# Decoder of two blocks on one core: shifts of the self attentions by blocks of eight heads, and a new table of turns

## Chip, cores, metric

One core of a Trainium2 chip runs the whole program in one launch; the other cores are idle. The metric is the time of one execution in microseconds, median of 3 runs.

## What is computed

Six layers with residuals over `x` of 4 batches, 256 tokens, 128 channels, each behind a layer norm:

```python
x = x + _L0_attn_ref(_layernorm(x), ...)            # 16 heads of 8, learned relative bias added after softmax
x = x + _L0_xattn_ref(_layernorm(x), ctx, ctx, ...) # 16 heads of 64, causal and padding masks
x = x + _L0_ffn_ref(_layernorm(x), ...)             # quantized linear, depthwise convolution, silu, quantized linear
x = x + _L1_attn_ref(_layernorm(x), ...)            # 16 heads of 4, causal, alibi
x = x + _L1_xattn_ref(_layernorm(x), ctx, ctx, ...) # attention between the 16 heads of each token
x = x + _L1_ffn_ref(_layernorm(x), ...)             # 8 experts, top 2, and a shared one
```

A self attention, of which the change speaks, is per batch and head

```python
attn = softmax(einsum('bhqd,bhkd->bhqk', q, k) * scale, axis=-1)
out = einsum('bhqk,bhkd->bhqd', attn + rel_bias, v)   # first block; the second has mask and alibi inside the softmax
```

## The kernel before

**Two lanes.** Lane A computes batches 0 and 1, lane B batches 2 and 3 (`NB` = 2 batches, `TT` = 4 tiles of 128 tokens each). Each lane has a region of SBUF, four PSUM banks (`bank[0]` to `bank[3]`, printed as A_banks and B_banks) and runs the stages l0a, l0x, ffn, l1a, l1x, moe one after the other. Weights and their quantization are a third program, W (`B_wq`), late loads a fourth, L.

**What sets the order.** Every stage gives one generator per engine; each `yield` ends a piece. `merged` (in `decoder`) joins the generators of an engine into its one queue by the string in `TURNS`: "A4 W1 A7" takes four pieces of lane A, one of the weights, seven of lane A. The numbers behind `yield` are not read by it (only `interleaved`, inside a stage, sorts by them). Engines wait for one another by semaphores, and nothing overtakes in a queue.

**Self attention, l0a and l1a** (class `Attention`, L176 to L358; the stages `rel_attention` and `alibi_attention`).

1. Normalization: VectorE takes statistics, GpSimd the power (`rstd`, L159), VectorE applies it (L164). TensorE transposes the tokens (L172), and at the very start of l0a also the context (L633), which a DMA brings (L464).
2. Projection per token tile (L647). Queries and keys are split into three bf16 parts each by VectorE (L566, L569) and GpSimd (L487, L490), then stacked in the rows of `stack`, queries by GpSimd (L496), keys by ScalarE (L531). TensorE transposes the stacks (L662, 16 steps `n` of four), and they are copied to `qkT` by VectorE (L459) or, every fourth, by ScalarE (L511). GpSimd clears the stack's space and `vals` beforehand (L477 to L482). In l1a the stacks are transposed at L1585 and copied at L1491 and L1495.
3. Maxima: TensorE computes scores with queries in rows (`tensor_S_pair` L296 for the first 16 heads of l0a, two heads at a time in both halves of the array; `tensor_S`, L226, for the others; L231 and L234 in l1a), VectorE takes minus the maximum of each row (L324). `JOBS` is 16 in l0a and 12 in l1a per batch.
4. Shift: when all 16 heads of a batch have their maximum, VectorE splits it into three bf16 parts (`vector_parts`, L339 to L348), TensorE transposes them (L242), VectorE copies (`vector_shiftT`, L352), and SP sends them by DMA into three rows of the queries (`sync_shift`, L252), so that the next scores come out with the maximum subtracted.
5. Loop over `U` = 32 heads: scores with keys in rows (L310; L262 to L266 in l1a), exponential on ScalarE (L358), products with the values per four heads (L286), output transposed and normalized.

```python
self.s_mx = st.sem("max_done", NB * self.JOBS)
if h == 0:
    pe.wait_ge(*self.s_q(16 * self.G * (b + 1)))
done, now = (min(jobs, k * jobs // (H - EARLY)) for k in (h, h + 1))
```

The first batch's maxima all stand before the loop; those of the second batch are spread over the first twelve heads of the loop (`ahead`, L361, with `EARLY` = 4), and its shift follows at head 12.

## Time and profile before

| | us |
|---|---|
| runs | 624.28, 620.47, 622.31 |
| median | 622.31 |
| the profiled execution's own time | 619.47 |
| its span | 617.5 |
| TensorE busy | 529.0 |
| VectorE busy | 424.6 |
| ScalarE busy | 323.5 |
| GpSimd busy | 192.1 |
| mean granted TensorE clock | 0.954 |

The span is from the first to the last instruction of the profiled execution; its own time is 2 us more. Busy times are of instructions that work; waits for semaphores and issuing of DMAs are not in them. The idle time of an engine is the span less its busy time.

### The profile page before, as it was taken

The page shows a single profiled execution, that of the slowest core. Times are in us where ns is not written, and L with a number is a line of the kernel's source. Part 1 is how long each engine was busy: PE and PEld are TensorE (multiplying, and loading weights), DVE is VectorE, ACT ScalarE, POOL GpSimd, SP SyncE. Part 2 cuts the span into 40 slices and gives each one's busy share as a digit, 9 for nine tenths or more (in the row PEclk, how much of TensorE's full clock was granted, in tenths as well). Part 3 has the DMA queues.
Part 4 walks back from the last instruction along what each step waited for, and adds up shares of the span by engine and source line. Part 5 has one row for each costly group of instructions (what it writes and reads, how often), then busy time and mean ns, then how long its engine had stood idle before and what let it go on. Part 6 is the DMA issues. An engine that isn't in the chain of part 4 may idle for free. (4 is left out here: it accounts for less than half of the span.)

```text
span 617.5 us, 12861 instructions
## 1 busy us (share of the span) xinstructions
PE 529.0 (86%) x4880; PEld 327.9 (53%) x4890; DVE 424.6 (69%) x1037; ACT 323.5 (52%) x807; POOL 192.1 (31%) x288
## 2 busy tenths in 40 slices
PE   2668787999999999778986489978988999999894
PEld 1433343344555656446554355766666867655453
DVE  6885764654463654798779876847557577889994
ACT  1423445567576674695733536554666555362440
POOL 3743200043245443432620031001113122435653
PEclk9965999999999999989997889999999999999998
DMA  8700000000030000000256005300000000303001
GB/s 299 267 1 2 2 2 3 1 3 2 1 136 3 1 1 1 2 2 1 80 143 243 3 17 156 97 11 3 4 2 2 3 3 1 138 2 137 2 1 34
DMA packets 25815, 27.92 MB, mean 45 GB/s; under 512 B 18177, under 2 KB 22794, under 8 KB 24858
## 3 DMA queue, kind: packets, MB, share of 16 engines
q1 hardware_dynamic: 25754, 27.10, 13.1%
q8 instruction: 39, 0.64, 0.4%
q14 instruction: 22, 0.18, 0.1%
HBM read 22.14 MB, written 4.75 MB: 44 GB/s over the span
## 5 line engine op out<-in xcount | busy, mean ns | idle before, releaser
L811 POOL TENSOR_TENSOR A_l0x_prob<-A_l0x_prob,A_l0x_inverted_sums 128x256 f32<-128x256 f32 (+1 forms) x32 | 25.9, 829 | 56.6 <-DVE A_l0x_inverted_sums L922 56.6
L811 POOL TENSOR_TENSOR B_l0x_prob<-B_l0x_prob,B_l0x_inverted_sums 128x256 f32<-128x256 f32 (+1 forms) x32 | 26.5, 848 | 45.1 <-DVE B_l0x_inverted_sums L922 45.1
L2080 PE MATMUL B_banks<-B_moe_xT,w_moe_rows 128*128 128x512 f32 x72 | 33.8, 596 | 1.7 <-DVE B_moe_h L2047 1.7
L2080 PE MATMUL A_banks<-A_moe_xT,w_moe_rows 128*128 128x512 f32 x72 | 34.3, 597 | 0.0
L324 DVE TENSOR_REDUCE B_l0a_nmax<-B_banks 128x2 f32<-128x512 f32 x32 | 21.4, 688 | 15.2 <-PE B_banks L226 11.9
L905 DVE TENSOR_REDUCE A_l0x_nmax<-A_banks 128x2 f32<-128x256 f32 (+1 forms) x32 | 16.3, 552 | 22.6 <-PE A_banks L980 22.5
L358 ACT ACTIVATE A_l0a_expT<-A_banks 128x512 f32<-128x512 f32 x32 | 18.3, 599 | 22.0 <-PE A_banks L310 22.0
L829 ACT ACTIVATE B_l0x_prob<-B_banks,B_l0x_nmax 128x128 f32<-128x128 f32 x64 | 26.0, 420 | 5.9 <-DVE B_l0x_nmax L905 5.7
L324 DVE TENSOR_REDUCE A_l0a_nmax<-A_banks 128x2 f32<-128x512 f32 x32 | 21.3, 688 | 9.8 <-PE A_banks L226 8.0
L829 ACT ACTIVATE A_l0x_prob<-A_banks,A_l0x_nmax 128x128 f32<-128x128 f32 x64 | 26.1, 425 | 1.7 <-DVE A_l0x_nmax L905 1.7
L846 ACT ACTIVATE A_l0x_probT<-A_banks 128x384 f32<-128x384 f32 x32 | 15.8, 493 | 19.3 <-PE A_banks L992 19.1
L846 ACT ACTIVATE B_l0x_probT<-B_banks 128x384 f32<-128x384 f32 x32 | 15.7, 490 | 15.9 <-PE B_banks L992 15.8
L324 DVE TENSOR_REDUCE B_l1a_nmax<-B_banks 128x2 f32<-128x512 f32 (+1 forms) x24 | 16.2, 689 | 9.9 <-PE B_banks L234 9.7
L358 ACT ACTIVATE B_l0a_expT<-B_banks 128x512 f32<-128x512 f32 x32 | 18.6, 601 | 8.2 <-PE B_banks L310 8.1
L358 ACT ACTIVATE A_l1a_expT<-A_banks 128x384 f32<-128x384 f32 x32 | 15.3, 494 | 14.5 <-PE A_banks L266 14.5
L358 ACT ACTIVATE B_l1a_expT<-B_banks 128x384 f32<-128x384 f32 x32 | 15.5, 491 | 14.0 <-PE B_banks L266 13.9
L1976 ACT ACTIVATE B_moe_h<-B_banks,w_moe_rest_rows 128x512 f32<-128x512 f32 x18 | 12.3, 686 | 19.7 <-PE B_banks L2080 19.6
L2080 PEld LDWEIGHTS B_banks<-B_moe_xT,w_moe_rows 128*128 128x128 f32 x72 | 12.8, 190 | 14.7 <-issue 12.0
L905 DVE TENSOR_REDUCE B_l0x_nmax<-B_banks 128x2 f32<-128x256 f32 (+1 forms) x32 | 16.2, 548 | 5.9 <-PE B_banks L980 5.9
L1709 POOL TENSOR_TENSOR A_l1x_prob<-A_l1x_prob,A_l1x_rz 128x512 f32<-128x512 f32 x8 | 8.3, 1042 | 38.2 <-DVE A_l1x_rz L1790 38.2
L1976 ACT ACTIVATE A_moe_h<-A_banks,w_moe_rest_rows 128x512 f32<-128x512 f32 x18 | 12.1, 680 | 13.8 <-PE A_banks L2080 13.7
L992 PE MATMUL B_banks<-w_const_rows,B_l0x_prob 128*128 128x128 f32 x96 | 16.6, 283 | 3.0 <-POOL B_l0x_prob L811 1.4
(609 smaller groups left out, 1570.7 us busy)
## 6 DMA issues: line engine op xcount, KB each, us to landing
w_toeplitz_rows<-in_toeplitz_rows SPq DMA_DIRECT2D x1, 3072.0 KB, 15.3
w_moe_rows<-in_moe_rows SPq DMA_DIRECT2D x1, 2304.0 KB, 9.6
w_l1x_rows<-in_l1x_rows SPq DMA_DIRECT2D x1, 2048.0 KB, 7.8
A_l1x_values<-A_l1a_v_tokens SPq DMA_DIRECT2D x4, 512.0 KB, 3.5
A_l1x_v_groups<-A_l1x_values SPq DMA_DIRECT2D x16, 128.0 KB, 3.1
B_l1x_values<-B_l1a_v_tokens SPq DMA_DIRECT2D x4, 512.0 KB, 3.5
B_l1x_v_groups<-B_l1x_values SPq DMA_DIRECT2D x16, 128.0 KB, 3.1
w_l0x_vo_rows<-in_l0x_vo_rows SPq DMA_DIRECT2D x1, 1024.0 KB, 9.0
```

Of the source, the lines that this page charges most:

```text
L324: dve.tensor_reduce(out, scores, AX, ALU.max, negate=True).then_inc(self.s_mx.sem, 1)
L358: act.activation(self.expT[:, u % self.ring, :], self.exp_bank(u)[:, 0:self.W], ACT.Exp, scale=self.scale).then_inc(self.s_p.sem, 1)
L811: ins = pool.tensor_tensor(pair, pair, bcast(rz[:, g % 2, i, :], 2, n), ALU.mult)
L829: ins = act.activation(prob[:, u % RING, at:at + n], bank[u % 2][:, at:at + n], ACT.Exp, bias=nmax[:, b, i, h:h + 1], accum_out=zsum[:, g ...
L846: act.activation(probT[:, u % 4, :], bank[2][:, 0:W], ACT.Copy).then_inc(s_pt.sem, 1)
L905: ins = dve.tensor_reduce(nmax[:, b, i, 2 * c:2 * c + 2], lane.banks[:, 0:2, at:at + n], AX, ALU.max, negate=True)
L992: ins = pe.transpose(bank[2][:, c * P:(c + 1) * P], prob[:, u % RING, c * P:(c + 1) * P], w["ident"][:])
L1709: pool.tensor_tensor(pr, pr, bcast(rz[:, n % 2, :], BL, 64), ALU.mult).then_inc(s_pn.sem, 1)
L1976: act.activation(h1[:, n % 2, :], hidden_bank(2 * n)[:, :], ACT.Identity, bias=w["moe_b1"][:, e, part:part + 1]).then_inc(s_h1.sem, 1)
L2080: pe.matmul(hidden_bank(k)[:, :], w["moe_w3" if which else "moe_w1"][:, ORDER[i], part, :], xT[:], start=True, stop=True).then_inc(s_h.sem, 1)
```

## The change

- **Blocks of eight heads** (`HB` = 8) take the place of batches in the shift: maxima, parts, transpose, copy and DMA are done for each of 4 blocks per lane and stage (`JOBS` is 8 in l0a, 6 in l1a, per block). `parts` and `shiftT` are double buffers over the blocks, with waits for their reuse.
- **How far ahead**: `due(n)` says how many score sets are issued by step `n` of the loop, `AHEAD` = 12 heads ahead. Before the loop stand `first` = 12 sets in l0a and 9 in l1a, of which the last 4 (3) come behind the first block's shift. A later block's shift is sent four steps before its first exponential.
- `tensor_S_pair` is gone; all heads' maxima scores come from `tensor_S`.
- **Stack copies** of the steps from `n` = 8 on are all ScalarE's (10 of 16 instead of 4); each is issued behind one set of scores.
- **Start of l0a**: TensorE transposes the tokens ahead of the context, ScalarE copies them in that order, and the context goes through `bank[3]`; the wait for it moves to the second stack transpose. GpSimd clears `vals` and the stack first and then computes `rstd`.
- **New turns** for all engines. Operations outside the two self attentions are the same; ScalarE's queue gets 10 table loads where it had 8.

```diff
-EARLY = 4
+HB = 8
+AHEAD = 12
...
-        self.jobs = [job for h in range(0, H, 4) for job in ((1, h, 2), (1, h + 2, 2), (0, h, 4))] if causal else [(None, h, 1) for h in range(H)]
+        self.jobs = [job for h in range(0, HB, 4) for job in ((1, h, 2), (1, h + 2, 2), (0, h, 4))] if causal else [(None, h, 1) for h in range(HB)]
+        self.BLOCKS = U // HB
+        self.first = self.due(-1)
...
+    def due(self, n):
+
+        return min(self.BLOCKS * self.JOBS, -(-(n + 1 + AHEAD) * self.JOBS // HB))
...
+    def completed(self, n):
+
+        k = self.due(n) // self.JOBS
+        return k - 1 if n >= 0 and k * self.JOBS > self.due(n - 1) else None
...
+        rows, n = P // self.G, HB // self.G
+        b, first = k * HB // H, k * HB % H // self.G
         for j in range(self.G):
-            dst = self.queries(b)[rows * j + self.row:rows * j + self.row + 3]
-            src = self.shiftT[32 * j:32 * j + 3 * self.columns, b, :]
+            dst = self.queries(b)[rows * j + self.row:rows * j + self.row + 3, first:first + n, :]
+            src = self.shiftT[32 * j:32 * j + 3 * n, k % 2, :]
             sp.dma_start(dst, src).then_inc(self.s_q.sem, 16)
...
-        if h == 0:
-            pe.wait_ge(*self.s_q(16 * self.G * (b + 1)))
+        if u % HB == 0:
+            pe.wait_ge(*self.s_q(16 * self.G * (u // HB + 1)))
+        if u == 0:
+            pe.wait_ge(*self.s_mx(self.first))
...
-    by_scalar = [n % 4 == 3 for n in range(STEPS)]
+    by_scalar = [n % 4 == 3 or n >= 4 * SB for n in range(STEPS)]
...
     def gpsimd(pool):
-        yield 2.0
-        w.loaded(pool, "const")
+        yield 0.0
         w.ready(pool, lane, "arena")
-        norm.gpsimd_rstd(pool)
-        yield 1.6
-        w.ready(pool, lane, "x")
-        yield 2.1
+        pool.memset(vals[:], 0.0).then_inc(s_init.sem, 1)
         pool.memset(stack[:, :, 0, :, 6 * HD:SW], 0.0)
...
+        yield 2.0
+        w.loaded(pool, "const")
+        norm.gpsimd_rstd(pool)
...
     def tensor(pe):
-        yield 0.0
+        yield 4.5
         w.loaded(pe, "const")
         w.ready(pe, lane, "arena")
+        tensor_transpose_tiles(pe, w, bank[0], xn, s_xn, s_xTp)
+        yield 5.5
         pe.wait_ge(*s_ctx(16))
...
-            if u % 2 == 0:
-                a.tensor_S_pair(pe, u)
-            else:
+            if u == a.JOBS:
+                a.tensor_shift(pe, 0)
+                yield SCORES + 1.2 * u + 0.8
+            a.tensor_S(pe, u)
+            if 4 * SB + u < STEPS:
                 yield
-                transpose_stack(4 * SB + u // 2)
+                transpose_stack(4 * SB + u)
...
-        "A4 W1 A7 W1 A20 B1 A4 B1 A1 B1 A3 B1 A3 B1 A3 B1 A1 B1 A1 B1 A3 B1 A2 B2 A3 B1 A2 B2 A5 B2 A2 B1 A3 B1 A2 B2 A5 B3 A2 B3 A3 B1 A3 B1 A1 B4 A4 B1 A2 B2 "
+        "A4 W1 A5 W1 A20 B1 A1 B1 A2 B1 A2 B1 A6 B2 A3 B1 A1 B2 A4 B1 A4 B1 A1 B1 A1 B1 A3 B1 A5 B2 A3 B3 A1 B1 A2 B1 A1 B1 A1 B2 A3 B3 A2 B1 A4 B1 A1 B1 A6 B1 "
...
```

The table of turns moves most instructions. Three places, each of before and of the change, rows as they stand in the queue of the engine (names of the program's tiles; `x4` is four in a row):

GpSimd's queue from lane A's third token tile on, before (`split` the parts of queries and keys, `expT` the space in which the stacks are built, `vals` the values, `rstd` the norm's factor):

```order
L487 CAST A_l0a_split<-A_l0a_rest_qk 128x256
L490 TENSOR_TENSOR A_l0a_split<-A_l0a_rest_qk,A_l0a_split 128x256
L496 COPY A_l0a_expT<-A_l0a_split 128x16x16 x2
L496 COPY A_l0a_expT<-A_l0a_split 128x16x8 x2
L159 TENSOR_TENSOR B_l0a_rstd<-B_l0a_ve,w_const_rows 128x4
L487 CAST A_l0a_split<-A_l0a_rest_qk 128x256
L490 TENSOR_TENSOR A_l0a_split<-A_l0a_rest_qk,A_l0a_split 128x256
L496 COPY A_l0a_expT<-A_l0a_split 128x16x16 x2
L496 COPY A_l0a_expT<-A_l0a_split 128x16x8 x2
L477 MEMSET B_l0a_expT 128x4x16x16
L478 MEMSET B_l0a_expT 128x4x16x13
```

and with the change:

```order
L499 CAST A_l0a_split<-A_l0a_rest_qk 128x256
L502 TENSOR_TENSOR A_l0a_split<-A_l0a_rest_qk,A_l0a_split 128x256
L484 MEMSET B_l0a_vals 128x3072
L485 MEMSET B_l0a_expT 128x4x16x16
L486 MEMSET B_l0a_expT 128x4x16x13
L487 MEMSET B_l0a_expT 128x4x16x3
L489 MEMSET B_l0a_vals 128x64
L508 COPY A_l0a_expT<-A_l0a_split 128x16x16 x2
L508 COPY A_l0a_expT<-A_l0a_split 128x16x8 x2
L499 CAST A_l0a_split<-A_l0a_rest_qk 128x256
L502 TENSOR_TENSOR A_l0a_split<-A_l0a_rest_qk,A_l0a_split 128x256
```

Lane B's five clears now stand between the split of lane A's third tile and its stack, and lane B's `rstd` behind the split of the fourth.

TensorE's queue around the first shift of lane A, before (`parts` the shift's parts, L242 its transpose, L310 the exponentials' scores, L226 and L296 the maxima's, L662 stack transposes, L647 the projection):

```order
L296 MATMUL A_banks<-A_l0a_qkT 128x256 x4
L647 MATMUL B_banks<-w_l0a_rows,B_l0a_xT 128x384
L662 MATMUL A_banks<-w_ident_bf,A_l0a_expT 128x128 x4
L242 MATMUL A_banks<-w_ident_bf,A_l0a_parts 128x128 x2
L647 MATMUL B_banks<-w_l0a_rows,B_l0a_xT 128x384
L310 MATMUL A_banks<-A_l0a_qkT 128x256 x4
L226 MATMUL A_banks<-A_l0a_qkT 128x256 x2
L662 MATMUL B_banks<-w_ident_bf,B_l0a_expT 128x128 x4
```

and with the change (L264 the shift's transpose, L327 the exponentials' scores, L248 the maxima's, L677 stack transposes, L660 the projection):

```order
L677 MATMUL A_banks<-w_ident_bf,A_l0a_expT 128x128 x4
L248 MATMUL A_banks<-A_l0a_qkT 128x256 x2
L173 MATMUL B_banks<-w_const_rows,B_l0a_xn 128x128 x4
L677 MATMUL A_banks<-w_ident_bf,A_l0a_expT 128x128 x4
L649 MATMUL B_banks<-w_const_rows,B_l0a_rest_qk 128x128 x4
L264 MATMUL A_banks<-w_ident_bf,A_l0a_parts 128x128 x2
L248 MATMUL A_banks<-A_l0a_qkT 128x256 x2
L660 MATMUL B_banks<-w_l0a_rows,B_l0a_xT 128x384
L248 MATMUL A_banks<-A_l0a_qkT 128x256 x4
L660 MATMUL B_banks<-w_l0a_rows,B_l0a_xT 128x384
L248 MATMUL A_banks<-A_l0a_qkT 128x256 x2
L327 MATMUL A_banks<-A_l0a_qkT 128x256 x4
```

The shift is transposed behind eight sets of scores, and four more sets, one head each, stand between it and the first exponentials.

ScalarE's queue where lane A's experts begin beside lane B's second cross attention (`moe_sigmoid` needs another table of functions than `l1x_prob`), before:

```order
L1740 ACTIVATE B_l1x_probT<-B_banks 128x512
L1744 ACTIVATE B_l1x_prob<-B_l1x_prob 128x512
L1982 ACT_TABLE_LOAD
L1982 ACTIVATE A_moe_sigmoid<-A_moe_gate 128x512
L1976 ACTIVATE A_moe_h_165<-A_banks,w_moe_rest_rows 128x512 x2
L1733 ACTIVATE B_l1x_keysT<-B_banks 128x4x128
```

and with the change:

```order
L1763 ACTIVATE B_l1x_prob<-B_l1x_prob 128x512
L2001 ACT_TABLE_LOAD
L2001 ACTIVATE A_moe_sigmoid<-A_moe_gate 128x512
L1995 ACTIVATE A_moe_h_165<-A_banks,w_moe_rest_rows 128x512
L1752 ACTIVATE B_l1x_keysT<-B_banks 128x4x128
L1759 ACTIVATE B_l1x_probT<-B_banks 128x512
L1763 ACT_TABLE_LOAD
L1763 ACTIVATE B_l1x_prob<-B_l1x_prob 128x512
```

An exponential of lane B (L1763) now stands behind lane A's first sigmoid, with a table load before it, and the next sigmoid takes another.

## Rows read from the trace of the kernel before

**Rows 1.** Part 1 of the page: engine busy us (share of the span) xinstructions.
```profile
PE 529.0 (86%) x4880; PEld 327.9 (53%) x4890; DVE 424.6 (69%) x1037; ACT 323.5 (52%) x807; POOL 192.1 (31%) x288
```

**Rows 2.** Windows: stretch, length, busy us (xinstructions) by engine, PEclk, DMA share, GB/s.
```profile
0.00:50.00 50.00, 26.71 (x169) 15.97 (x170) 36.01 (x87) 15.55 (x42) 27.92 (x54) 0.85 0.49 175
50.00:100.00 50.00, 41.69 (x429) 20.31 (x429) 30.91 (x75) 23.27 (x56) 6.25 (x14) 0.84 0.01 2
300.00:350.00 50.00, 36.34 (x266) 23.72 (x265) 40.29 (x103) 21.91 (x58) 11.52 (x38) 0.92 0.46 144
```

**Rows 3.** Timeline of TensorE, 0 to 50 us: start us, us, what [idle before].
```profile
9.71 1.09 PE L633 MATMUL A_banks<-w_const_rows,A_l0a_rest_qk 128*128 128x128 f32 x4 [9.71 <-DMA A_l0a_rest_qk<-in_ctx]
...
13.01 2.90 PE L647 MATMUL A_banks<-w_l0a_rows,A_l0a_xT 128*128 128x384 f32 x4 [0.78 <-ACT A_l0a_xT L518]
...
43.43 0.27 PE L242 MATMUL A_banks<-w_ident_bf,A_l0a_parts 128*128 128x128 bf16 x2 [0.73 <-ACT A_l0a_qkT L511]
...
47.24 0.39 PE L310 MATMUL A_banks<-A_l0a_qkT 64*128 64x256 bf16 x4 [2.83 <-DMA A_l0a_qkT<-A_l0a_shiftT]
```

**Rows 4.** Timeline of VectorE, 0 to 50 us.
```profile
6.79 4.77 DVE L164 TENSOR_SCALAR A_l0a_xn<-A_x,A_l0a_mv,A_l0a_rstd 128x128 f32<-128x128 f32 x4
...
26.32 1.29 DVE L324 TENSOR_REDUCE A_l0a_nmax<-A_banks 128x2 f32<-128x512 f32 x2
...
27.52 0.41 DVE L459 COPY A_l0a_qkT<-A_banks 128x512 bf16<-128x512 bf16 x1
...
41.07 1.29 DVE L324 TENSOR_REDUCE A_l0a_nmax<-A_banks 128x2 f32<-128x512 f32 x2 [0.37 <-PE A_banks L296]
...
43.74 0.29 DVE L352 COPY A_l0a_shiftT<-A_banks 128x256 bf16<-128x256 bf16 x1 [0.16 <-PE A_banks L242]
```

**Rows 5.** Timeline of GpSimd, 0 to 30 us.
```profile
5.70 1.05 POOL L159 TENSOR_TENSOR A_l0a_rstd<-A_l0a_ve,w_const_rows 128x4 f32<-128x4 f32 x1 [5.26 <-DVE A_l0a_ve L155]
...
6.71 0.94 POOL L477 MEMSET A_l0a_expT<- 128x1024 bf16 x1
...
11.46 0.23 POOL L482 MEMSET A_l0a_vals<- 128x64 f32 x1
...
23.87 1.21 POOL L496 COPY A_l0a_expT<-A_l0a_split 128x256 bf16<-128x256 bf16 x4
...
28.59 1.21 POOL L496 COPY A_l0a_expT<-A_l0a_split 128x256 bf16<-128x256 bf16 x4
```

**Rows 6.** Timeline of VectorE, 110 to 115 us.
```profile
112.76 1.11 DVE L164 TENSOR_SCALAR A_l0a_xn<-A_l0a_xn,A_l0a_mv,A_l0a_rstd 128x128 f32<-128x128 f32 x4
```

**Rows 7.** Timeline of VectorE, 325 to 350 us.
```profile
328.99 1.71 DVE L1495 COPY A_l1a_kT<-A_banks 32x512 bf16<-32x512 bf16 x4
...
348.41 0.29 DVE L352 COPY A_l1a_shiftT<-A_banks 128x256 bf16<-128x256 bf16 x1
```

**Rows 8.** Timeline of TensorE, 350 to 355 us.
```profile
352.91 0.40 PE L262 MATMUL A_banks<-A_l1a_qT,A_l1a_kT 128*128 128x256 bf16 x1 [1.01 <-DMA A_l1a_qT<-A_l1a_shiftT]
```

**Rows 9.** Timeline of TensorE, two places in lane A's first loop.
```profile
64.14 0.39 PE L226 MATMUL A_banks<-A_l0a_qkT 64*128 64x256 bf16 x2
64.46 0.44 PE L706 MATMUL A_banks<-w_const_rows,A_l0a_xT 128*128 128x128 f32 x2
...
88.88 0.39 PE L296 MATMUL B_banks<-B_l0a_qkT 64*128 64x256 bf16 x4
89.11 0.38 PE L310 MATMUL A_banks<-A_l0a_qkT 64*128 64x256 bf16 x4
```

**Rows 10.** Timeline of ScalarE, 340 to 342 us.
```profile
340.00 1.28 ACT L1114 ACT_TABLE_LOAD   x1
341.30 1.72 ACT L1114 ACTIVATE B_ffn_conv<-B_ffn_conv 128x512 f32<-128x512 f32 x3
```

**Rows 11.** Tiles A_l0a_qkT and A_l0a_shiftT: durations ns min/median/max, first and last start us.
```profile
L310 PE MATMUL A_banks<-A_l0a_qkT x64: 266/279/417, 47.2 to 98.3; 64*128 64x256 bf16 x64
...
L252 SPq DMA_DIRECT2D A_l0a_qkT<-A_l0a_shiftT x4: 698/710/887, 44.1 to 76.3; - x4
```

More of the change, by code:

```diff
@@ L216, in tensor_S @@
     def tensor_S(self, pe, m):
-        b, at = divmod(m, self.JOBS)
-        c, h, n = self.jobs[at]
+        b, c, h, n = self.job(m)
         bank = self.score_bank(m)
-        if b:
+        if m == self.JOBS or m >= self.first:
             pe.wait_ge(*self.s_mx(m))
@@ L223, in tensor_S @@
             pe.wait_ge(*self.s_mx(m - 1))
+        if self.shifted is not None and bank is self.bank[0]:
+            pe.wait_ge(*self.s_shT(self.shifted + 1))
+            self.shifted = None
         if c is None:
@@ L288, in tensor_PV @@
         ins.then_inc(self.s_pv.sem, 1)
-    def tensor_S_pair(self, pe, m):
-        if m:
-            pe.wait_ge(*self.s_mx(m))
-        for c in range(SB):
-            for h in (m, m + 1):
-                ins = pe.matmul(self.score_bank(h)[:, c * S:(c + 1) * S], self.q(0, h, c * P, P), self.k(0, h, 0, S),
-                                start=(c == 0), stop=True, skip_group_check=True)
-                if c == SB - 1:
-                    ins.then_inc(self.s_s.sem, 1)
     def tensor_E_pair(self, pe, u):
         b, h = divmod(u, H)
-        if h == 0:
-            pe.wait_ge(*self.s_q(16 * self.G * (b + 1)))
+        if u % HB == 0:
+            pe.wait_ge(*self.s_q(16 * self.G * (u // HB + 1)))
+        if u == 0:
+            pe.wait_ge(*self.s_mx(self.first))
         if u:
@@ L315, in vector_max @@
     def vector_max(self, dve, m):
[L316 to L317 removed]
+        b, c, h, n = self.job(m)
         bank = self.score_bank(m)
@@ L358, in scalar_exp @@
         act.activation(self.expT[:, u % self.ring, :], self.exp_bank(u)[:, 0:self.W], ACT.Exp, scale=self.scale).then_inc(self.s_p.sem, 1)
-def ahead(n, jobs):
-    b, h = divmod(n, H)
-    if b + 1 >= NB:
-        return range(0)
-    done, now = (min(jobs, k * jobs // (H - EARLY)) for k in (h, h + 1))
-    return range(jobs * (b + 1) + done, jobs * (b + 1) + now)
 def split_columns(part_of):
@@ L535, in scalar @@
                 copy_stack(act, scalar_copy, 4 * t - 1)
-        for n in (STEPS - 5, STEPS - 1):
-            yield SCORES + 1.2 * (2 * n - 4 * TT + 1) + 0.2
+        for n in range(4 * SB, STEPS):
+            yield SCORES + 1.2 * (n - 4 * SB) + 0.8
             copy_stack(act, scalar_copy, n)
@@ L671, in tensor @@
                     transpose_stack(n)
-        for u in range(a.JOBS):
+        for u in range(a.first):
             yield SCORES + 1.2 * u - 0.4
@@ L694, in tensor @@
                 a.tensor_E_pair(pe, n)
-            for i, u in enumerate(ahead(n, a.JOBS)):
+            for i, u in enumerate(range(a.due(n - 1), a.due(n))):
                 yield LOOP + STEP * (n + 0.5 * i) - 0.5
@@ L1348, in sync @@
                     sp.dma_start(vg[64 * half:64 * (half + 1), to:to + P // 16, :], src[half, j]).then_inc(s_vg, 16)
-        for b in range(NB):
-            yield SCORES + 3.0 + 0.75 * a.JOBS + 2.0 if b == 0 else LOOP + STEP * (b * H - EARLY + 1)
-            a.sync_shift(sp, b)
+        for k in range(a.BLOCKS):
+            yield SCORES + 3.0 + 0.75 * a.JOBS + 2.0 if k == 0 else LOOP + STEP * (k * HB - 3)
+            a.sync_shift(sp, k)
     def gpsimd(pool):
@@ L1587, in tensor @@
             ins.then_inc(s_stT.sem, 1)
-        for u in range(a.JOBS):
+        for u in range(a.first):
             yield SCORES + 3.0 + 0.75 * u - 0.4
@@ L1604, in tensor @@
                 a.tensor_E(pe, n)
-            for i, u in enumerate(ahead(n, a.JOBS)):
+            for i, u in enumerate(range(a.due(n - 1), a.due(n))):
                 yield LOOP + STEP * (n + 0.5 * i) - 0.5
```

166 lines of the change are left out of this document (89 added, 77 removed), and 42 rows, old and new, of the table TURNS.

## Prediction

> **What bounds the kernel now.** I read the engine shares first: TensorE is busy for 86% of the span [rows 1], so beside it everything else is mostly cover, and the other 88.5 us (617.5 - 529.0) are all that a better order can win back. Then the stretches [rows 2] say where they lie: TensorE does 26.7 us of work in the first 50 us and 41.7 in the next 50, at a mean granted clock of 0.85 and 0.84; from 300 to 350, where both lanes stand around the second self attention, only 36.3. So 31.6 us of the idle time lie before 100 us and 13.7 in 300 to 350, over half of it in a quarter of the span. The chain of waits that ends the program is of no use here: it reaches back only over the last 14 us. What decides are the starts of the two self attentions, in which one lane has little to do and the other has not caught up.
>
> Lane A's start is a serial story [rows 3]. TensorE first waits 9.71 us for the context tokens, projects from 13.01, and after the last of 16 score sets transposes the shift at 43.43; the first matmul of the loop of exponentials comes at 47.24, after 2.83 us of waiting for the shift's DMA. In between VectorE sets the pace [rows 4]: 8 pairs of maxima from 26.32 to 42.36, 2.0 us a pair, 1.29 of it the two maxima and 0.41 the stack copy that stands in the same queue. GpSimd [rows 5] clears lane A's buffers after the first rstd (6.71 to 11.69), and while it does so VectorE's four normalizations take 4.77 us [rows 4]; the same four take 1.11 us later [rows 6].
>
> **The change part by part**, as lane A meets it.
>
> 1. *Buffers cleared ahead, tokens ahead of the context.* The five clears (4.98 us, [rows 5]) move in front of rstd. GpSimd has nothing before 5.70, so they end about when x's variance is there, and rstd keeps its time. The normalizations no longer run beside them: 6.79 + 1.11 = 7.9 instead of 11.56. But the context is still transposed before the first projection on TensorE's queue and still lands at 9.71; its four transposes take 1.09 [rows 3], so the projection starts near 10.8 instead of 13.01: **-2.2 us** on this chain. Token transposes and xT (ScalarE) are done by then.
>
> 2. *GpSimd's new turn for lane B's clears.* Before, lane B's clears follow all four q stacks of lane A, the last of which ends at 29.80 [rows 5]. Now they stand between the split and the stack of lane A's third token tile. That stack would end 2.2 us earlier than 25.08, at 22.9; the clears are the same five as lane A's, 4.98, so it ends near 27.9, the fourth (4.72 us behind it before, 29.80 - 25.08, of which some waiting for its split falls away, while lane B's rstd, 1.05 like lane A's, is put in between) near 31. Every score set but the first is queued on TensorE behind a stack transpose of these tiles, so the scores cannot run ahead of them.
>
> 3. *Eight maxima instead of sixteen before the shift, and ScalarE copies the stacks.* Eight maxima at 0.65 (1.29/2) are 5.2 us, with no copy between. Sets 4 to 7 follow the fourth stack at 31: the last maximum ends near 34.5 where it ended at 42.36. Parts, transpose and shift copy then take what they took (42.39 to 44.03), the DMA its 3.2 us (47.24 - 44.03), although it carries half the bytes; I take no gain from these. **The loop starts near 39.5 instead of 47.24: -7.7 us.** Four sets and their maxima (0.3 us of TensorE each) move from before it into the loop or under the DMA: +0.7, leaving **-7.0**. Bounds: -4 if lane B's clears wait for the quantized weights and push the stacks on, -10 if the stacks don't hold the scores.
>
> 4. *Lane B's start.* It has the same 4 sets fewer, but lane A's loop fills TensorE beside it (41.7 of 50). I count **-1** (0 to -4).
>
> 5. *Second self attention.* From the end of the key copies (330.7) to the shift copy (348.41) VectorE is full: 12 maxima, lane B's FFN and the parts [rows 7], while TensorE waits; its loop opens at 352.91 [rows 8]. Six maxima (6 x 0.65 = 3.9) leave this stretch for the loop, where VectorE should have idle time as in the first one (30.9 of 50 us busy beside lane A's first loop, [rows 2]). Lane B's convolution steps move ahead of the stack copies, which changes their place, not the sum. **-4** for lane A, **-1** for lane B, whose stretch has less idle time. Bounds for both: 0 and -7.
>
> 6. *What it adds.* Each stage and lane has two shifts more. TensorE: 16 transposes, two of them in 0.27 us [rows 3], **+2**. VectorE: two more blocks of four or five small operations and a copy, about 1.2 us a block if a small one takes 0.2 and the copy 0.29 [rows 4]; the first self attention gives 6 stack copies of 0.41 back per lane, so it adds nothing there, and 2.4 per lane in the second, under TensorE. 24 more DMAs on SP, 0.7 us each to issue [rows 11], on a queue that is nearly empty; none of them stands behind one that lands late except in the second self attention, where lane A's last two blocks queue behind lane B's value transfers.
>
> 7. *Unpaired scores.* The score sets of the first 16 heads came in pairs, four matmuls whose halves of the array overlap; now each head comes alone. In the loop of before two single matmuls hold TensorE for 0.32 us (64.14 to 64.46), four paired ones for 0.23 (88.88 to 89.11) [rows 9]. A pair of heads so costs 0.64 instead of 0.23 to 0.33. 16 pairs in both lanes: 16 x 0.35 = 5.6, of which lane A's half falls into idle time; **+2.5**.
>
> 8. *Two more table loads on ScalarE*, where lane A's experts start inside lane B's cross attention. A load takes 1.28 us, and the activation behind it starts 0.02 us later [rows 10]: 2.6 us on an engine that is busy half the time; I count 0 (bounds 0 and +2.6). The Trainium skill, "ScalarE: Activation LUTs", section "What ACT_TABLE_LOAD costs", counts a drain of some 1.38 us on top, 2.66 us a switch; the sum's upper bound by it would be +5.3, but the row shows no drain.
>
> Sum: -7.0 - 1 - 4 - 1 + 2 + 2.5 = **-8.5 us**. Against the profiled execution (span 617.5, its own time 619.47) that is 611.0; the median of the three runs is 622.31, 2.8 above it, so the same sum gives 613.8 for the median; between the two, and nearer the second, since it is medians that are compared, I say **613**. About 0.5% (3 us) is what a measurement of this kernel can tell from no change.
>
> **Rivals.**
> *R1, only the first start counts* (0.17). If the second attention's stretch stays bound by VectorE's same sum of work (B's FFN chain ends no earlier, and its extra 5 us of small operations land there), item 5 falls out: -8.5 + 5 = -3.5, 618.8 for the median. For it: VectorE is busy 9 of 10 there; against it: the six maxima really leave.
>
> *R2, the idle time is only moved and TensorE pays* (0.12). TensorE gets 2 + 5.6 us more work. If the lanes wait as long as before, because each block's shift is one more round trip (maximum, parts, transpose, copy, 3.2 us DMA) in front of TensorE's queue, four instead of two per lane and stage, the time is 619.5 + 7.6 = 627 for the profiled execution, 630 for the median, and 626 if half of the extra work is hidden. It decides if TensorE's idle time before 100 us stays over 29 us. Against it: in the loop a block's exponentials come four heads after its maxima, 6.4 us at 1.6 us a head (32 heads from 47.2 to 98.3, [rows 11]), and the round trip takes about 5.
>
> *R3, the whole order gets tighter* (0.15). The new turns are laid for all stages; if the lanes' better alignment also takes 5 to 8 us of the idle time in 250 to 450 us and at the end, 601 to 607. For it: idle time there is larger than what I use; against it: nothing in the operations of these stages changes.
>
> *R4, the change is not what it says*: the order of instructions shows eight-head blocks in both lanes and stages, so nothing is left for it.
>
> **Numbers.** My forecast has 0.56: its own range is 608 to 618. R3 takes the low end to 603, R1 with the small ends of items 3 and 5 (3.7 and 5 us less gained, so none is left) the high end to 623; R2 and the bottom of R3 are left out: 603 to 623. Faster by over 0.5% (below 619.2): 0.56, all of R3 and a third of R1, 0.76. Within 0.5% : 0.13. Slower (over 625.4): 0.11.
>
> **What would show it.** TensorE's first exponential matmul of lane A near 39.5 us, not 47.2; the first four normalizations 1.1 us in sum; TensorE's idle time before 100 us near 24 us; lane A's second loop some 12 us earlier than 352.9; TensorE's busy time up by 3 to 7 us. I am wrong if the stacks hold the scores past 37 us, or if the gain of the start is gone by 150 us because lane B arrives no earlier.

## The result, and the profile after

| | before | with the change |
|---|---|---|
| median of 4 runs, us | 622.24 | 614.23 |
| lowest to highest | 620.47 to 624.28 | 612.85 to 615.70 |
| ratio, 95% interval | | 0.987, 0.9832 to 0.9909 |
| the profiled execution's own time | 619.47 | 615.70 |
| its span | 617.5 | 613.9 |
| mean granted TensorE clock in it | 0.954 | 0.956 |

The spans of the two profiled executions are only 3.6 us apart, the medians 8.0: the profiled execution of before is faster than all runs of its column, the one after is the slowest of its own. That is itself a part of the result (the clock, below).

The first lines of the profile after: engine busy us, share of the span, xinstructions.

```profile
PE 533.2 (87%) x4906; PEld 330.1 (54%) x4906; DVE 426.0 (69%) x1069; ACT 330.8 (54%) x821; POOL 195.2 (32%) x288
```

TensorE has 4.2 us more to do than in [rows 1] and is idle 80.7 us instead of 88.5. The windows before 100 us (columns as in [rows 2]):

```profile
0.00:50.00 50.00, 31.71 (x190) 17.80 (x190) 32.97 (x87) 21.67 (x55) 28.16 (x54) 0.85 0.48 175
50.00:100.00 50.00, 41.81 (x449) 20.81 (x451) 32.60 (x82) 26.24 (x59) 6.28 (x14) 0.84 0.01 3
```

Idle time before 100 us fell from 31.6 to 26.5 us (50 - 31.71 + 50 - 41.81). Further on, windows of fixed times cut the two programs at different work. So the next ones are cut at three places of the program: where lane A's first loop opens, where lane B issues the last scores of its first loop, and where lane A's second loop opens. Before:

```profile
0.00:47.24 47.24, 24.77 (x153) 14.98 (x154) 34.46 (x84) 13.73 (x37) 26.04 (x49) 0.86 0.51 186
47.24:158.04 110.80, 100.02 (x916) 46.82 (x918) 64.16 (x170) 60.73 (x149) 21.61 (x38) 0.92 0.01 2
158.04:352.91 194.87, 166.97 (x1214) 104.19 (x1212) 135.87 (x359) 119.55 (x375) 66.77 (x112) 0.96 0.15 49
352.91:617.47 264.56, 237.22 (x2602) 161.96 (x2610) 190.09 (x424) 129.52 (x247) 77.70 (x90) 0.98 0.11 36
```

and with the change:

```profile
0.00:42.20 42.20, 24.90 (x144) 14.54 (x145) 27.48 (x73) 16.59 (x42) 25.28 (x46) 0.88 0.57 207
42.20:160.94 118.74, 108.30 (x974) 52.63 (x974) 72.51 (x198) 69.24 (x176) 24.59 (x44) 0.91 0.01 2
160.94:346.82 185.88, 159.23 (x1155) 99.02 (x1151) 130.38 (x347) 113.53 (x355) 66.89 (x109) 0.98 0.16 51
346.82:613.92 267.10, 240.82 (x2638) 163.90 (x2638) 195.67 (x454) 131.45 (x249) 78.49 (x90) 0.97 0.11 35
```

TensorE is idle 22.5, 10.8, 27.9 and 27.3 us in the four stretches before, and 17.3, 10.4, 26.7 and 26.3 now. So 5.2 of the 7.8 us stand ahead of lane A's first loop, 0.3 in the next stretch, 1.2 ahead of the second loop and 1.1 behind. Work moves too: up to lane B's last scores TensorE is busy 8.4 us more than before, in the stretch behind 7.7 us less.

TensorE at lane A's start, in its order of time, answers to [rows 3]:

```profile
7.36 1.16 PE L173 MATMUL A_banks<-w_const_rows,A_l0a_xn 128*128 128x128 f32 x4 [7.36 <-DVE A_l0a_xn L165]
10.29 1.11 PE L649 MATMUL A_banks<-w_const_rows,A_l0a_rest_qk 128*128 128x128 f32 x4 [1.77 <-DMA A_l0a_rest_qk<-in_ctx]
11.19 2.77 PE L660 MATMUL A_banks<-w_l0a_rows,A_l0a_xT 128*128 128x384 f32 x4
...
27.29 0.40 PE L677 MATMUL A_banks<-w_ident_bf,A_l0a_expT 128*128 128x128 bf16 x4 [3.26 <-POOL A_l0a_expT L508]
...
33.32 0.61 PE L677 MATMUL A_banks<-w_ident_bf,A_l0a_expT 128*128 128x128 bf16 x4
33.87 0.61 PE L248 MATMUL A_banks<-A_l0a_qkT 64*128 64x256 bf16 x2
...
35.48 1.11 PE L173 MATMUL B_banks<-w_const_rows,B_l0a_xn 128*128 128x128 f32 x4
...
37.67 0.42 PE L264 MATMUL A_banks<-w_ident_bf,A_l0a_parts 128*128 128x128 bf16 x2
...
40.92 0.39 PE L248 MATMUL A_banks<-A_l0a_qkT 64*128 64x256 bf16 x2 [0.40 <-DVE A_l0a_nmax L340]
42.20 0.39 PE L327 MATMUL A_banks<-A_l0a_qkT 64*128 64x256 bf16 x4 [0.89 <-DVE A_l0a_nmax L340]
```

The projection starts at 11.19 (13.01 before), the shift's transpose at 37.67 (43.43), the loop at 42.20 (47.24). GpSimd and VectorE in the same stretch, against [rows 5] and [rows 4]:

```profile
21.27 2.66 POOL L484 MEMSET B_l0a_vals<- 128x3072 f32 x1
...
26.03 1.21 POOL L508 COPY A_l0a_expT<-A_l0a_split 128x256 bf16<-128x256 bf16 x4
...
29.25 1.22 POOL L508 COPY A_l0a_expT<-A_l0a_split 128x256 bf16<-128x256 bf16 x4
```

```profile
6.87 1.11 DVE L165 TENSOR_SCALAR A_l0a_xn<-A_x,A_l0a_mv,A_l0a_rstd 128x128 f32<-128x128 f32 x4
...
23.33 2.57 DVE L156 TENSOR_SCALAR B_l0a_ve<-B_l0a_mv 128x4 f32<-128x4 f32 x1
...
35.59 0.69 DVE L340 TENSOR_REDUCE A_l0a_nmax<-A_banks 128x2 f32<-128x512 f32 x1 [0.39 <-PE A_banks L248]
```

In the second self attention lane A's loop opens at 346.82 ([rows 8]: 352.91):

```profile
341.97 0.37 PE L264 MATMUL A_banks<-w_ident_bf,A_l1a_parts 128*128 128x128 bf16 x2 [2.84 <-DVE A_l1a_parts L367]
346.82 0.40 PE L288 MATMUL A_banks<-A_l1a_qT,A_l1a_kT 128*128 128x256 bf16 x1 [2.02 <-DMA A_l1a_qT<-A_l1a_shiftT]
```

### The profile page after: what moved, and what is told of

Read it like the earlier page. It is cut to its first block, busy times and chain, and to the rows that moved or that the text cites. A ratio compares the mean times of both kernels' runs of the same rounds, so it can differ in the third digit from the quotient of the medians.

```text
span 613.9 us, 13013 instructions
## 1 busy us (share of the span) xinstructions
PE 533.2 (87%) x4906; PEld 330.1 (54%) x4906; DVE 426.0 (69%) x1069; ACT 330.8 (54%) x821; POOL 195.2 (32%) x288
## 3 DMA queue, kind: packets, MB, share of 16 engines
q1 hardware_dynamic: 25826, 27.10, 13.4%
## 4 chain that ended last, share of the span: by engine, by line
PE 64%; DVE 19%; ACT 6%; issue 4%; POOL 2%; DMA 2%; SPq 1%; POOLq 0%; DVEq 0%; ACTq 0%
PE B_banks L2099 5%; PE A_banks L2099 4%; PE A_banks L312 4%; PE B_banks L312 3%; PE A_banks L1021 2%; PE A_banks L1008 2%; DVE A_l0a_nmax L340 2%; PE A_banks L248 2%; PE A_banks L2131 1%; PE B_banks L1562 1%; PE A_banks L1824 1%; PE A_banks L957 1%; PE A_banks L1029 1%; PE A_banks L959 1%; PE B_banks L957 1%
## 5 line engine op out<-in xcount | busy, mean ns | idle before, releaser
L340 DVE TENSOR_REDUCE B_l0a_nmax<-B_banks 128x2 f32<-128x512 f32 x32 | 21.8, 686 | 15.3 <-PE B_banks L248 15.1
L862 ACT ACTIVATE A_l0x_probT<-A_banks 128x384 f32<-128x384 f32 x32 | 15.7, 492 | 15.6 <-PE A_banks L1008 15.5
L340 DVE TENSOR_REDUCE A_l1a_nmax<-A_banks 128x2 f32<-128x512 f32 (+1 forms) x24 | 16.3, 687 | 8.2 <-PE A_banks L256 8.2
L1995 ACT ACTIVATE B_moe_h<-B_banks,w_moe_rest_rows 128x512 f32<-128x512 f32 x18 | 12.2, 685 | 17.3 <-PE B_banks L2099 17.2
```

The costliest lines, as they stand in the source:

```text
L340: dve.tensor_reduce(out, scores, AX, ALU.max, negate=True).then_inc(self.s_mx.sem, 1)
L862: act.activation(probT[:, u % 4, :], bank[2][:, 0:W], ACT.Copy).then_inc(s_pt.sem, 1)
L1995: act.activation(h1[:, n % 2, :], hidden_bank(2 * n)[:, :], ACT.Identity, bias=w["moe_b1"][:, e, part:part + 1]).then_inc(s_h1.sem, 1)
```

## Experiments

The variants were measured on three chips, each beside the kernel before, whose median is 622.5 to 622.6 on every one of them; "the changed kernel" below is its second measurement, made on one of the three. **The changed kernel again**, for comparison:

> The changed kernel unaltered, as the measure for the variants on the same chip: 614 us, 0.985 to 0.991 of the kernel before.

Measured 614.05 (613.15 to 616.50), ratio 0.9884 (0.9854 to 0.9914). Lane A's first loop opens at 42.99 in its profile and the second at 347.5. So a start time of two executions of one kernel differs by 0.8 us, and smaller differences are not read below. From the opening of the second loop to the end both profiles take 267.1 us (spans 613.9 and 614.6).

### The blocks: nothing behind the shift

```diff
+    if lane.name == "A":
+        a.shift_at = a.first        # twelve sets instead of eight
...
-            if u == a.JOBS:
+            if u == a.shift_at:
                 a.tensor_shift(pe, 0)
...
+        if a.shift_at == a.first:
+            a.tensor_shift(pe, 0)
```

(the same for the parts and the copy on VectorE)

> The changed kernel with lane A's first shift in the first self attention behind all twelve sets of scores that stand before the loop, not behind eight. Theory of the blocks: what the blocks of eight heads give is that the sets behind the shift cover its way (parts, transpose, copy, 3.2 us of DMA); now nothing covers it, lane A's first exponential scores come 3.5 to 4 us later (46), and the time is 2 to 4 us more. Rival, it is the new turns and stack copies that give the start, and the block's size little: first exponential scores within 1.5 us of 42.2 and the time within 1 us.

Measured 620.87 (617.91 to 624.31), 6.8 above the changed kernel, ratio 0.9977 (0.9957 to 0.9998) to the one before. Its timeline of TensorE:

```profile
44.04 0.28 PE L265 MATMUL A_banks<-w_ident_bf,A_l0a_parts 128*128 128x128 bf16 x2 [1.48 <-DVE A_l0a_parts L368]
47.81 0.61 PE L328 MATMUL A_banks<-A_l0a_qkT 64*128 64x256 bf16 x4 [3.48 <-DMA A_l0a_qkT<-A_l0a_shiftT]
```

The loop opens 4.8 us later and TensorE stands 3.48 us before it for the DMA, which no set of scores covers. With the new turns and the new stack copies in place, lane A's first shift alone, put behind four more sets, takes nearly the whole gain back. The theory of the blocks holds, and was priced too low (2 to 4). But not all of the 6.8 is the block's. Some 2 us are the clock (mean over the runs 0.952, 0.959 in those of the changed kernel, at the 3.0 us per 0.01 found below). The profiles say the same in another way. Against the repeated run lane B's last scores of the first loop come 4.2 us later (166.05, 161.90), and that is the delay of the start; lane A's second loop opens 7.9 us later (355.47, 347.53), which is also the difference of the spans (622.5, 614.6). The 3.8 us between the two were lost on the way: 189.4 us from the one place to the other, where the changed kernel takes 185.9 and 185.6. Two more variants below, whose first loops open no later than the repeated run's, lose as much there (189.6 and 189.8). All three have 6.8 us at half clock (granted clock 0.50) at about 300 us, here

```profile
299.70:306.50 6.80, 5.68 (x35) 4.07 (x34) 3.88 (x17) 2.31 (x4) 1.76 (x3) 0.50 0.00 0
```

where the repeated run of the changed kernel has none:

```profile
288.40:343.00 54.60, 41.81 (x308) 25.70 (x306) 47.61 (x133) 27.33 (x74) 15.74 (x41) 1.00 0.41 127
```

So the sets behind the first shift are worth 4 to 5 us, and the rest of the 6.8 goes with a lower clock, which a changed order can bring without a later start. Whether the half clock is all of those 3.8 us was not tried.

> The changed kernel with lane A's first shift in the second self attention behind all nine sets that stand before the loop, not behind six. In the changed kernel the last of six maxima ends at 339.8, the loop opens at 346.8. Theory: three maxima of 0.65 us and what stands between them on VectorE move ahead of the shift, the loop opens 2 to 4 us later, the time is 1 to 3 us more. Rival, VectorE's sum of work in this stretch bounds it, and the order within it does not matter: the loop opens within 1 us of 346.8, the same time.

The same edit in the second self attention (lane A, nine sets instead of six). Measured 618.78 (615.42 to 623.91), 4.7 above. TensorE there:

```profile
344.50 0.29 PE L265 MATMUL A_banks<-w_ident_bf,A_l1a_parts 128*128 128x128 bf16 x2 [3.79 <-DVE A_l1a_parts L368]
349.27 0.40 PE L289 MATMUL A_banks<-A_l1a_qT,A_l1a_kT 128*128 128x256 bf16 x1 [4.48 <-DMA A_l1a_qT<-A_l1a_shiftT]
```

and its window:

```profile
300.00:350.00 50.00, 34.66 (x245) 21.32 (x243) 41.56 (x108) 22.26 (x53) 12.07 (x37) 0.95 0.47 144
```

The loop opens at 349.3 instead of 346.8 to 347.5, and TensorE is idle 15.3 us in this window instead of 11.6. From there on the program takes 267.1 us, as the changed kernel. So the profiles give the block of the second self attention 1.8 to 2.5 us (span 616.4 against 614.6 and 613.9); of the 4.7 between the medians some 1 is the clock (0.955 against 0.959), and the rest isn't explained. The order within VectorE's work matters; the rival falls.

### Clears, and what stands behind a late instruction

Lane A's clears behind its rstd again:

```diff
-        pool.memset(vals[:], 0.0)...; norm.gpsimd_rstd(pool)
+        norm.gpsimd_rstd(pool); pool.memset(vals[:], 0.0)...      # lane A only
```

> The changed kernel with lane A's five clears behind its rstd again, as before the change (lane B's stay where the change has them). Start theory: rstd stays near 5.7, the clears run beside the four normalizations of lane A, which take 4.8 us instead of 1.1; the projection starts at 13.0 instead of 11.2 and the first exponential scores 1.8 us later, the time is 1 to 2 us more: 615.5 to 616. Rival, it is hidden by what follows (GpSimd's stacks, lane B's clears): first exponential scores within 0.5 us of 42.2, 614.

Measured 618.45 (616.55 to 621.73), 4.4 above the changed kernel. VectorE's row of the normalizations:

```profile
6.82 4.48 DVE L165 TENSOR_SCALAR A_l0a_xn<-A_x,A_l0a_mv,A_l0a_rstd 128x128 f32<-128x128 f32 x4
```

4.48 us instead of 1.11, the projection at 12.8, the loop at 43.8. The mechanism is as I had it. The median moved by more than the start did, of which some 1.3 us go by the clock (0.955 against 0.959); the span of the profile is 1.0 us longer (615.6, 614.6).

Lane B's clears and rstd behind lane A's stacks (two pieces of lane B moved in the table of GpSimd's turns):

```diff
     "gpsimd":
-        "A11 B1 A3 B1 A2 B14 ...
+        "A15 B2 A1 B14 ...
```

> The changed kernel with lane B's five clears and its rstd on GpSimd's queue behind the stack of lane A's fourth token tile. In the changed kernel the clears run from 21.27 to 26.03 and the stack behind them ends at 27.2, with TensorE waiting 3.26 us for it. Queue theory: the third stack now ends near 22.5, the fourth near 26.5, the first exponential scores of lane A come at 39 to 40 instead of 42.2, and the time is 1 to 3 us below the changed kernel (611 to 613). Rival, the lead is lost to lane B, whose clears and rstd now end 2 to 3 us later, so that its normalizations and its loop start later: same time as the changed kernel, 614. Rival, TensorE sets the pace anyway (a transposed stack and a set of scores every 1.08 us at half clock): lane A's first scores move by less than 1 us.

Measured 617.99 (614.11 to 620.26), 3.9 above, with the loop opening at 44.92: none of the three. The stacks were done early, and then this, on TensorE and on VectorE:

```profile
25.04 0.38 PE L677 MATMUL A_banks<-w_ident_bf,A_l0a_expT 128*128 128x128 bf16 x4 [0.92 <-ACT A_l0a_vals L537]
...
35.55 0.61 PE L248 MATMUL A_banks<-A_l0a_qkT 64*128 64x256 bf16 x2 [5.22 <-DVE A_l0a_nmax L340]
```

```profile
32.83 2.06 DVE L165 TENSOR_SCALAR B_l0a_xn<-B_x,B_l0a_mv,B_l0a_rstd 128x128 f32<-128x128 f32 x4 [5.71 <-POOL B_l0a_rstd L160]
```

Lane B's normalizations stand on VectorE's queue between lane A's third and fourth maximum. Their rstd was now late, and lane A's maxima, ready to run, waited 5.7 us behind them. So I moved those too, behind the parts of lane A's first shift on VectorE, and lane B's transposes behind that shift and the ninth set on TensorE, whose queue changes like this:

```diff
 L677 MATMUL A_banks<-w_ident_bf,A_l0a_expT 128x128 x4
+L264 MATMUL A_banks<-w_ident_bf,A_l0a_parts 128x128 x2
+L248 MATMUL A_banks<-A_l0a_qkT 128x256 x2
 L173 MATMUL B_banks<-w_const_rows,B_l0a_xn 128x128 x4
 L649 MATMUL B_banks<-w_const_rows,B_l0a_rest_qk 128x128 x4
-L264 MATMUL A_banks<-w_ident_bf,A_l0a_parts 128x128 x2
-L248 MATMUL A_banks<-A_l0a_qkT 128x256 x2
```

> As in the run with lane B's clears behind lane A's stacks, and besides lane B's normalizations on VectorE behind the parts of lane A's first shift, and lane B's token and context transposes on TensorE behind that shift and one set of scores. Head-of-line theory: the 5.7 us that lane A's maxima lost in that run came only from lane B's normalizations standing before them on VectorE's queue while their rstd was late. Now the eighth maximum ends near 33.3, the first exponential scores of lane A come at 39 to 40 (42.2 in the changed kernel), lane B's tokens are transposed at 35.5 as there, and the time is 1 to 3 us below the changed kernel. Rival, lane A's lead is worth nothing since lane B fills TensorE later: first exponential scores at 39 to 40, and the time of the changed kernel. Rival, stacks and clears were not what held lane A: first exponential scores at 42.

Measured 617.03 (612.66 to 617.36), ratio 0.9909 (0.9876 to 0.9941), which overlaps the changed kernel's. In its profile the shift is transposed at 34.18 (38.33 in the repeated run of the changed kernel), and lane B issues the last scores of its first loop at 158.9 (161.9), 3.0 us ahead. But lane A's second loop opens at 348.7 (347.5), and these are its windows, and then the repeated run's:

```profile
250.00:300.00 50.00, 37.61 (x281) 25.48 (x283) 39.46 (x101) 31.54 (x92) 17.06 (x24) 0.90 0.00 1
300.00:350.00 50.00, 36.62 (x253) 22.86 (x253) 41.46 (x108) 23.32 (x54) 11.68 (x37) 0.93 0.48 145
```

```profile
250.00:300.00 50.00, 36.78 (x298) 24.75 (x296) 40.80 (x104) 32.82 (x98) 16.48 (x23) 0.97 0.00 1
300.00:350.00 50.00, 38.35 (x264) 23.97 (x264) 43.39 (x117) 23.36 (x55) 12.52 (x37) 0.93 0.47 145
```

Up to 300 us the clock is lower (0.90, 0.97), up to 350 TensorE is idle 13.4 us instead of 11.6. The lead is gone before the second loop: this is the second of the variants with 6.8 us at half clock near 300 us (189.8 us from lane B's last scores to lane A's second loop, 185.6 in the repeated run). The head-of-line theory is right about the start (the eighth maximum ends at 32.72, and the transpose comes 4.1 us earlier), and the rival right about the time: a lead of 3 us at 160 us isn't carried to the end here. The loop itself opened at 41.45 only, not at 39 to 40, since the last of the twelve maxima now waits for sets that stand behind lane B's projections.

### The added work, the copies, the table loads

Every transpose of a shift three times:

```diff
-            ins = pe.transpose(view[...], self.parts[:, k % 2, c, :], ...)
+            for again in range(3):
+                ins = pe.transpose(view[...], self.parts[:, k % 2, c, :], ...)
```

> The changed kernel with every transpose of a shift issued three times, 64 more transposes on TensorE than the change has. At 0.13 us each (0.27 us for two) they are 8.6 us of TensorE. If TensorE bounds the program all through the loops: +7 to +9 us, 621 to 623, and the 16 transposes of the change cost 2 us as I summed them. If they fall into idle time of the starts or under waits for banks: +3 to +5, and they cost about 1.

Measured 616.64 (615.70 to 619.66), 2.6 above for 64 transposes, and less than either forecast; the interval of its ratio, 0.992 (0.9894 to 0.9946), overlaps the changed kernel's. But these transposes stand in groups that are there anyway. All shifts' transposes together are busy 4.93 us in the repeated run (32 of them) and 9.60 here (96): 0.07 us for one more in a group, not 0.13. The change adds groups: eight of two transposes, and TensorE's rows of them go from 2.24 to 5.07 us. So the run shows that a longer group is cheap, and not that the change's 16 transposes are.

Score pairs head by head, in the kernel before:

```diff
-        for c in range(SB):
-            for h in (m, m + 1):
+        for h in (m, m + 1):
+            for c in range(SB):
```

> The kernel before with the two heads of a score pair one after the other (the same matmuls, order head by head), which takes the overlap of the two halves of the array away and nothing else. My term: 16 pairs in both lanes at 0.35 us, lane A's half hidden, +2.5 us, 624.5 to 625; TensorE's busy time up by up to 5.6 us. Lower bound: the pairs wait for the maxima anyway, no difference (622). Upper bound: +5.6.

Measured 622.31 (619.69 to 624.43), ratio 1.0 (0.9981 to 1.002): the lower bound. TensorE is busy 529.8 us instead of 529.0, and the same row of its timeline, in this kernel and then in the one before:

```profile
26.16 0.40 PE L296 MATMUL A_banks<-A_l0a_qkT 64*128 64x256 bf16 x4 [0.97 <-ACT A_l0a_qkT L511]
```

```profile
25.91 0.39 PE L296 MATMUL A_banks<-A_l0a_qkT 64*128 64x256 bf16 x4 [0.97 <-ACT A_l0a_qkT L511]
```

Four matmuls take 0.40 us one head after the other and 0.39 paired. Two take 0.39 ([rows 9]): in so short a group the time is the same whatever the number. The Trainium skill ("TensorE: Matmul & The Clock Gate", section "Step-by-step: what each phase is for") says that an isolated matmul cannot hide its drain, and that one in a stream costs about its columns alone. By that page I should not have divided a group's time by its count, as I did for the transposes; the trace agrees as far as the fixed part of a group goes.

For the same reason this run doesn't price what the change does. It leaves the four matmuls of two heads in one group; the change makes two groups of two of them, with a stack transpose behind each. At half clock a group of four held TensorE for 0.54 us before, up to the next row:

```profile
29.44 0.61 PE L296 MATMUL A_banks<-A_l0a_qkT 64*128 64x256 bf16 x4 [1.05 <-DVE A_l0a_nmax L324]
29.98 0.61 PE L662 MATMUL A_banks<-w_ident_bf,A_l0a_expT 128*128 128x128 bf16 x4
```

and a group of two holds it for the same 0.54 us with the change:

```profile
31.70 0.61 PE L248 MATMUL A_banks<-A_l0a_qkT 64*128 64x256 bf16 x2
32.24 0.61 PE L677 MATMUL A_banks<-w_ident_bf,A_l0a_expT 128*128 128x128 bf16 x4
```

In the whole program the 128 matmuls for the maxima of the first self attention are busy 7.88 (pairs) and 13.76 us (single heads) before, and 24.71 with the change (columns: PE, PEld, PEclk, DMA share, GB/s):

```profile
0.00:618.00 618.00, 7.88 (x64) 2.61 (x64) 0.95 0.14 45
0.00:618.00 618.00, 13.76 (x64) 4.11 (x64) 0.95 0.14 45
0.00:618.00 618.00, 24.71 (x128) 8.15 (x128) 0.96 0.14 45
```

That is 3.1 us more. A run of the changed kernel with its score pairs in one group would price them in time; there is none.

VectorE's stack copies as before, in the changed kernel:

```diff
-    by_scalar = [n % 4 == 3 or n >= 4 * SB for n in range(STEPS)]
+    by_scalar = [n % 4 == 3 for n in range(STEPS)]
```

> The changed kernel with ScalarE copying every fourth stack step only, so that VectorE copies six more per lane, each behind a maximum. VectorE then spends 0.69 + 0.41 = 1.10 us for a set of scores and a copy, and TensorE 1.08 us (0.54 + 0.54 at half clock) for what it issues between. Theory of balance: lane A's first exponential scores come 0.5 to 1 us later, the time is within 1 us of the changed kernel (614 to 615). Rival, VectorE paces the start: 6 copies of 0.41 us are all added, 2.5 us later, 616 to 617.

Measured 616.60 (614.79 to 619.28), while lane A's loop opens at 42.66, as in the repeated run (42.99). The start did not move, so VectorE does not pace it. Of the 2.5 us more, some 2 are what the lower mean clock of these runs (0.952 against 0.959) makes at 3.0 us per 0.01. Its profile is the third with 6.8 us at half clock near 300 us: 189.6 us from lane B's last scores to lane A's second loop, after a start that is as early as the changed kernel's.

Eight table loads instead of ten (lane A's first sigmoid behind lane B's exponential L1763, two pieces moved in ScalarE's turns):

> The changed kernel with lane A's first sigmoid and the expert step behind it moved on ScalarE's queue to behind lane B's last exponential but none, so that 8 table loads are left of 10. My term: two loads of 1.28 us on an engine that is busy half the time cost nothing, and the sigmoid comes 4 us later: within 0.5 us of the changed kernel (614). Rival, the loads are on the path: -1 to -2.6. Rival, the later sigmoid holds up the experts: +1 to +3.

Measured 614.47 (613.11 to 616.87), ratio 0.9885 (0.9855 to 0.9915): no difference from the changed kernel.

### Halves of the change

The old and the new form of each self attention side by side in one program, the table of turns joined at 285 us:

```diff
-                stages = (... lambda: alibi_attention(lane, w, x[i], cT[i], keep), ...)
+                stages = (... lambda: alibi_attention_old(lane, w, x[i], cT[i], keep), ...)
```

> The changed first self attention with the second one of before; the turns are those of the change for every piece that it starts before 285 us, and those of before from there on. Parts theory: the idle time of TensorE before 100 us falls by 5 us as in the changed kernel (26.5 instead of 31.6), the first self attention costs 1 us for 8 transposes and 2 us for unpaired scores, and the idle time of 300 to 360 us stays that of before, so half of the gain is there: 618 us, 4 below the kernel before. Rival, only the first start counts: 614 to 615, as the whole change. Rival, the early gain is not carried over to the end without the new second half: 621 to 623.

Measured 623.61 (619.68 to 625.76), ratio 1.0014 (0.9991 to 1.0037).

> The first self attention and its turns of before up to 285 us, then the changed second self attention with the turns of the change. Parts theory: lane A's loop opens about 4 us after 347 us (the lead that the first start gave is missing), TensorE's idle time in 300 to 360 us falls by 4 us against before, 8 transposes cost 1 us: 618 to 619 us. Rival, only the first start counts: 621 to 623. Rival, the second attention gives all of it: 614 to 616.

Measured 624.89 (624.03 to 626.43), ratio 1.0048 (1.0028 to 1.0068). Neither half is faster than the kernel before, though the whole is, and lane A's second loop opens at 357.57 and 354.65, later than before (352.91). The rivals that gave 621 to 623 come nearest, and both programs are slower than that. In the first of the two, the early gain is there (idle time before 100 us 25.3), and lane B's first cross attention, which ends at 306.8 in the changed kernel and at 314.0 before, ends at 318.1. The last rows of it are those of the kernel before, 4.1 us later (307.66 there for the first of these):

```profile
311.78 1.03 PE L1763 MATMUL A_banks<-A_ctxT,w_l1x_rows 128*64 128x256 f32 x8
312.65 0.82 PE L1021 MATMUL B_banks<-B_l0x_probT,B_l0x_vals 128*64 128x256 f32 x8
313.40 1.12 PE L1758 MATMUL A_banks<-w_l1x_rows,A_ctxT 128*128 128x512 f32 x2
314.36 3.73 PE L1029 MATMUL B_banks<-w_l0x_vo_rows,B_l0x_qT 128*128 128x128 f32 x32
```

I read this as the old turns putting lane A's projections, from the joint on, before what lane B, now ahead, could have run; no run shows it. These two runs don't price the halves: a joined table is a third order, laid for neither. They show that the lead of the first start was worth nothing with this joint.

## Why the prediction held

The number held (614.2 against 613), and in part by luck. The sum had 13 us of gain and 4.5 us of cost. The profiled pair has 7.8 us less idle time and 4.2 us more work, 3.6 us in all; between the medians some 3 us of clock come on top, which the sum didn't contain, and scatter.

| term | forecast | what the runs show |
|---|---|---|
| 1, clears and tokens ahead | -2.2 | projection 1.8 earlier; with the clears put back 1.0 more by the profiles, 4.4 by the medians |
| 2, stacks held by lane B's clears | third at 27.9, fourth near 31 | 27.24 (26.03 + 1.21) and 30.47 |
| 3, lane A's loop | 39.5, -7.0 | 42.20, -5.0 |
| 4, lane B's loop | -1 | opens at 88.95 instead of 98.45, last scores at 160.94 instead of 158.04 |
| idle time before 100 us | near 24 | 26.5 (31.6) |
| 5, second self attention | -5 | loop 6.1 earlier, idle time between lane B's last scores and this loop down by 1.2 |
| 6, 16 transposes and more | +2 | 2.8 busy in TensorE's rows (2.24, 5.07) |
| 7, unpaired scores | +2.5, of 5.6 on TensorE | 3.1 busy in TensorE's rows (21.6, 24.7) |
| 8, two table loads | 0 | 0 |
| TensorE's clock | not in the sum | about -3 |

**Steps 1 and 2** were right in mechanism and size. Lane B's clears hold the third stack, and TensorE waits 3.26 us for it.

**Step 3 was too large, most of it in the maxima.** I took eight maxima at VectorE's 0.65 us each; the last five came every 1.08 us, since TensorE issues a stack transpose and a set between two of them and both took 0.54 at half clock (33.32, 33.87, then 34.40). The eighth ended at 36.28, not 34.5: 1.8 of the 2.7 us by which the loop missed 39.5. And I counted the four sets behind the shift as +0.7, partly under the DMA. They stand in part behind lane B's projections on TensorE's queue, and the first exponential waits for all twelve maxima: the release at 42.20 is the maximum, not the DMA. That the sets do cover the DMA is shown by the run with the shift behind them (47.8).

**Step 4** was far off for the place and not for the whole. Lane B's loop opens 9.5 us earlier, outside the bounds of 0 to -4, but it then shares TensorE with lane A's, which still ends within 1.5 us of before, and its own last scores come 2.9 us later. My sign of being wrong, the gain of the start gone by 150 us, was written for a lane B that arrives no earlier; the lanes' times alone don't decide it. TensorE's idle time does: up to lane B's last scores it is 5.5 us less than before, and up to lane A's second loop 6.8.

**Step 5 failed in size.** The loop opens 6.1 us earlier and not the 12 that steps 3 and 5 make together. Of these, 5.5 us of idle time were won by lane B's last scores, and this stretch adds 1.2 where I had 5. That is closer to rival R1 (only the first start counts) than to my term. The block is still worth something there, as the nine-set run shows (1.8 to 2.5 us by the profiles, 4.7 by the medians); what takes back the rest was not tried.

**Steps 6 and 7.** The costs did come on TensorE: the two groups of rows are busy 5.9 us more, in part beside other matmuls, and TensorE as a whole 4.2, near the 4.5 of the sum and inside the 3 to 7 that I named as a sign. The two runs that I made for them (three transposes for one, pairs head by head) changed what is inside a group, while the change adds groups. So what the two terms cost in time, beside a gain in the waits, stays open. R2's sign of 29 us idle before 100 us did not appear (26.5): TensorE does pay, but the idle time was not only moved.

**The clock** was not in the sum. In 75 runs of the kernel before, on three chips, the mean granted clock is 0.940 to 0.955 and the time 618.6 to 625.3; a line through them has 3.0 us per 0.01. Their mean clock is 0.949, that of ten runs of the changed kernel 0.959: some 3 of the 8 us. That the new order brings the higher clock about is likely, and not shown apart from it: the two profiled executions have nearly the same clock (0.954 and 0.956) and the same in the first 100 us, and there the gain is only 3.6 us of span.

The half clock does not explain the 4.2 us of busy time. In the stretches whose granted clock is 0.50 TensorE is busy 42.3 us in both profiles: 24.8 before 100 us and 15.7 from 250 to 400 in the kernel before, 28.4 and 11.5 with the change. Between the medians the clock's 3 us come on top of the 3.6, and the remainder of the 8 is scatter of the two profiled executions in their runs.

## What to carry to other kernels

Cut a serial preparation into blocks so that something remains to issue behind each transfer: four sets of scores behind the shift were worth 4 to 5 us here, the largest single effect (6.8 between the medians, the rest through the clock). When a step is made early or late in one engine's queue, look at what is queued behind its consumers on the next engine; one late rstd held another lane's maxima for 5.7 us. Price short matmuls by their groups and not by their number, and let an experiment add the groups that the change adds: two matmuls held TensorE as long as four. And before a start that moved is given as the cause of a new time, compare the clock of the stretches behind it: a variant whose start didn't move was 2.5 us slower.
